# Attention values: per-head matrices against Wv, 64x64 weighing tiles and Wo

## What is computed

```
def mha(xq, ctx, wq, wk, wv, wo, bo):
    q, k, v = (heads of) xq @ wq, ctx @ wk, ctx @ wv
    attn = softmax(q k^T / sqrt(64))
    out = attn v                     # per head, then side by side: [.., 1024]
    return out @ wo + bo
x0 = layernorm(x)
h1 = adaln(x0);  y1 = mha(h1, h1, ...) + x0
h2 = adaln(y1);  y2 = mha(h2, context, ...) + y1
h3 = adaln(y2);  x1 = x + y2 + glu_ff(h3)
n  = layernorm(x1)
out = x1 + sum over the top 2 of 8 experts of score * (silu(a) * g) @ w2[e].T,   a, g = n @ w1[e].T
```

## Time and profile before

| | before |
|---|---|
| median of 3 runs | 2113.37 us (2111.95 to 2113.82) |
| profiled execution, first to last instruction | 2124.9 us |
| PE busy, weight loads busy | 2039.6 us, 1337.7 us |
| DVE, ACT, POOL busy | 1323.4, 1386.2, 1071.9 us |
| granted clock of PE, mean | 0.991 |
| DMA | 127.35 MB, 60 GB/s |

### The profile page before, as it was taken

How to read it: one execution, slowest core, us unless ns; L and a number is a source line. 1 busy time by engine, 2 the same in 40 slices (tenths; PEclk the granted TensorE clock), 3 DMA queues, 4 the chain that set the end, 5 groups by cost and what they waited for, 6 DMA issues and landing times. The chain is left out here.

```text
span 2124.9 us, 38735 instructions
## 1 busy us (share of the span) xinstructions
PE 2039.6 (96%) x11068; PEld 1337.7 (63%) x11068; DVE 1323.4 (62%) x3389; ACT 1386.2 (65%) x2659; POOL 1071.9 (50%) x1198
## 2 busy tenths in 40 slices
PE   7899999999999999999999999999999889899996
PEld 5455555555555555555555565555555558799996
DVE  5554657676767676767676666666656545455565
ACT  4566666676667676767676767676766666566663
POOL 2444444636363637363737373737363445556664
PEclk9999999999999999999999999999999999999998
DMA  4110111121111111111111111111122312222256
GB/s 153 45 26 25 50 35 51 46 50 45 49 45 50 46 53 45 49 45 49 45 49 45 49 45 51 47 48 52 44 54 64 96 48 57 58 56 72 60 185 215
DMA packets 136321, 127.35 MB, mean 60 GB/s; under 512 B 14665, under 2 KB 110569, under 8 KB 136234
## 3 DMA queue, kind: packets, MB, share of 16 engines
q1 hardware_dynamic: 127466, 109.11, 18.7%
q0 software_dynamic: 8768, 17.20, 2.5%
HBM read 86.63 MB, written 40.67 MB: 60 GB/s over the span
## 5 line engine op out<-in xcount | busy, mean ns | idle before, releaser
L1928 POOL TENSOR_TENSOR pr<-pr,sm 128x512 f32<-128x512 f32 x256 | 277.7, 1098 | 483.7 <-DVE sm L1462 483.7
L1126 ACT ACTIVATE kp<-ps 128x512 f32<-128x512 f32 x512 | 298.9, 601 | 179.5 <-PE ps L283 176.2
L834 PE MATMUL ps<-tt,V 128*128 128x512 f32 x768 | 380.3, 593 | 3.5 <-ACT tt L1126 3.5
L1452 DVE TENSOR_REDUCE mx<-ps 128x8 f32<-128x512 f32 x256 | 176.8, 691 | 306.3 <-PE ps L783 306.3
L1126 ACT ACTIVATE tt<-ps 128x512 f32<-128x512 f32 x512 | 275.2, 591 | 40.2 <-PE ps L813 39.6
L783 PE MATMUL ps<-kp,hf 128*64 128x256 f32 x2048 | 276.8, 392 | 6.9 <-DVE pr L1455 3.9
L283 PE MATMUL ps<-cT,M 128*128 128x512 f32 x768 | 262.0, 464 | 0.0
L783 PEld LDWEIGHTS ps<-kp,hf 128*64 128x64 f32 x2048 | 124.4, 136 | 196.9 <-DVE pr L1455 142.4
L1126 ACT ACTIVATE pt<-ps 128x512 f32<-128x512 f32 x256 | 153.6, 600 | 141.4 <-PE ps L795 139.1
L283 PE MATMUL ps<-hk,M 128*128 128x512 f32 x768 | 242.2, 438 | 0.0
L941 PE MATMUL ps<-xT,wt 128*128 128x128 f32 (+1 forms) x1728 | 221.9, 278 | 4.0 <-DVE wt L1753 4.0
(11 more groups left out here) (235 smaller groups left out, 3470.3 us busy)
## 6 DMA issues: line engine op xcount, KB each, us to landing
mod<-emb_s SPq DMA_DIRECT2D x96, 256.0 KB, 4.3
xr<-rows_s SPq DMA_DIRECT2D x144, 66.0 KB
cb<-y_s SPq DMA_DIRECT2D x32, 256.0 KB
x_in<-in_x_dram SPq DMA_DIRECT2D x16, 256.0 KB, 4.4
xn_s<-x_in SPq DMA_DIRECT2D x16, 256.0 KB, 2.1
res<-xn_s SPq DMA_DIRECT2D x16, 256.0 KB, 2.8
c_in<-in_ctx_dram SPq DMA_DIRECT2D x16, 256.0 KB, 4.7
y_s<-res SPq DMA_DIRECT2D x16, 256.0 KB, 2.0
```

The costliest lines, as they stand in the source:

```text
L834: mm = nc.tensor.matmul(psO[:], Vw[a][:, g * HG + head_at(h), :], tt[:, h, :], start=(g == 0 and h == 0), stop=ends)
L1126: return nc.scalar.activation(o, i, ACT.Copy)
L1452: nc.vector.tensor_reduce(mx[:, p % 2, :], heads(psS[p % 2][:]), AX_X, ALU.max).then_inc(max_done, 1)
L1928: tensor(v, v, sm[:, p, :].unsqueeze(2).broadcast_to([P, HG, 64]), ALU.mult).then_inc(prob_done, 1)
```

## The change

- Setup no longer multiplies Wv with Wo. Wv is kept as two float32r halves (WV0, WV1), Wo as it is (WO0, WO1).
- `values`: the values of a tile for eight heads, 3 matmuls of 512 columns, 4 tiles per unit; ACT copies them to vp.
- `weigh`: 64 matmuls per unit, each 64 rows, 64 stationary columns, 64 moving columns, in two groups (pairs) of four heads; the row halves go to two banks, the column halves to two halves of the partitions. ACT copies four banks to os.
- `project`: 16 matmuls with a 128x128 tile of os stationary and 128 columns of Wo moving; the result has rows as partitions, so oT, back1 and back2 of the attentions go. The bias is added to the residual rows by POOL (`add_bias`), the residual rows have tiles of their own (y1r, y2r).
- No float32r splits of tt and no copy h_tm, c_tm.
- Order on PE in a slot: four turns, two weighings, four scores, four projections, four values, then the key products with the stages and GLU products. The four turned tiles have banks of their own and ACT and DVE copy two each. Banks are dealt anew: scores in psum 0, 3, 4, 5, the feed-forward's sum in psum 6, the rings, now of keys and values, again 6, 6, 4 and 3 banks.

```diff
+            def values(i, u, t, bank):
+                a, g = divmod(u, 2)
+                src = hk if a == 0 else cT
+                mm3(bank[:], lambda k: src[:, k, t * P:(t + 1) * P], lambda k: WV[a][:, k, g * CT:(g + 1) * CT]).then_inc(v_done, 1)
             def weigh(i, u, pair):
-                for s in range(2):
-                    rows = slice(64 * s, 64 * s + 64)
-                    nc.tensor.matmul(pst[s][:], tm[rows, p, :], pt[rows, p % 2, :], start=True, stop=True).then_inc(t_done, 1)
+                if pair == 0:
+                    pe.wait_ge(vp_done, v_count(i, u, NT - 1))
+                    wait(turned(i, u, 0))
+                    wait(turned(i, u, 1))
+                else:
+                    for w in left_in(i, u, WEIGHED[3]):
+                        wait(w)
+                for t in range(NT):
+                    if pair == 0 and t > 1:
+                        wait(turned(i, u, t))
+                    if t == 0 or pair == 0 and t > 1:
+                        pe.sem_inc(seen, 1)
+                    for j in range(2):
+                        for odd in range(2):
+                            h = 4 * pair + 2 * j + odd
+                            g, c = divmod(h, HH)
+                            for e in range(2):
+                                keep = slice(64 * e, 64 * e + 64)
+                                mm = nc.tensor.matmul(WEIGHED[2 * pair + e][64 * odd:64 * odd + 64, 256 * j + 64 * t:256 * j + 64 * t + 64], vp[keep, t, 64 * h:64 * h + 64],
+                                                      pt[keep, t, c * P + 64 * g:c * P + 64 * g + 64], start=True, stop=True)
+                mm.then_inc(w_done, 1)
             def project(i, u, j):
-                    mm = nc.tensor.matmul(psO[:], Vw[a][:, g * HG + head_at(h), :], tt[:, h, :], start=(g == 0 and h == 0), stop=ends)
+                if j % 2 == 0:
+                    wait(weighed(i, u, j + 1))
+                for t in range(NT):
+                    mm = nc.tensor.matmul(psO[:, t * D:(t + 1) * D], os[:, j, t * P:(t + 1) * P], WO[a][:, HH * g + j, :],
+                                          start=(g == 0 and j == 0 and t == 0), stop=(g == 1 and j == HH - 1 and t == NT - 1))
...
             def slot(i, u):
+                if last:
+                    for p in range(NT):
+                        if p == NT - 1 and u == 3 and ok(i - 2) and not c_last(i - 2):
+                            pe.wait_ge(glu, FT * (i - 2) + 1)
+                        if p == NT - 1 and u == 0 and ok(i - 3):
+                            pe.wait_ge(glu, FT * (i - 2))
                         turn(li, lu, p)
+                if u == 0 and ok(i - 3) and not c_last(i - 3):
+                    glu_down(i - 3, FT - 1)
+                if last:
+                    for pair in range(2):
+                        weigh(li, lu, pair)
+                if here:
+                    for p in range(NT):
                         scores(i, u, p)
+                if last:
+                    for j in range(HH):
+                        project(li, lu, j)
+                if here:
+                    for t in range(NT):
+                        product("v", t)
                 for h in range(HG):
                     if then:
-                        next_key(h)
+                        product("k", h)
...
-                    if last and h >= 2:
-                        project(li, lu, h - 2)
```

On the other engines:

```diff
             def slot(i, u):          # ACT
+                if last:
+                    for p in (0, 2):
+                        turn_out(li, lu, p)
+                if u == 0 and ok(i - 3):
+                    out_glu(i - 3)
+                if last:
+                    for b in range(4):
+                        weighed_out(li, lu, b)
                 if here:
+                    for p in range(NT):
+                        exp(i, u, p)
+                    for t in range(NT):
+                        values_out(i, u, t)
...
             def slot(i, u):          # DVE
+                if last:
+                    for p in (1, 3):
+                        turn_out(li, lu, p)
                 for p in range(NT):
...
+                if here:
+                    total(i, u, 2)
+                    total(i, u, 3)
```

More of the change, by code:

```diff
@@ L777, in scores @@
                         pe.wait_ge(hx_hi[1], i)
-                if not (isinstance(n, int) and n < 2):
-                    pe.wait_ge(sub_done, n - 1)
+                elif live(*before(i, u)):
+                    wait(weighed(*before(i, u), p - 1))
+                bank = SCORED[p][:].rearrange("p (c s k) -> p c s k", c=HH, s=2)
                 for s in range(2):
                     cols = slice(p * P + 64 * s, p * P + 64 * s + 64)
-                    for j in range(2):
-                        mm = nc.tensor.matmul(psS[p % 2][64 * j:64 * j + 64, :].rearrange("p (h s k) -> p h s k", h=HH, s=2)[:, :, s, :],
-                                              hf[u // 2][:, cols], kp[:, j * HH:(j + 1) * HH, cols], start=True, stop=True)
-                        if s == 1:
-                            mm.then_inc(s_done, 1)
@@ L1005, in next_key @@
-                def next_key(h):
-                    if h < len(RINGS[u]):
-                        bank = RINGS[u][h]
-                        if last:
-                            for w in [(pt_done, 4 * seq(li, lu) + 4)] if bank is psT else [] if bank in psS else t_free(li, lu, 3 if bank is psH else 2):
-                                wait(w)
-                        if here and bank in psS:
-                            pe.wait_ge(sub_done, 4 * seq(i, u) + 4)
-                    keys(*after(i, u), h)
@@ new lines, in slot, with product @@
+                if last:
[3 more added lines that the diff above has]
+                    for p in range(NT):
+                        scores(i, u, p)
+                if last:
+                    for j in range(HH):
+                        project(li, lu, j)
+                def product(kind, x):
+                    made, banks = products(i, u), RINGS[u]
+                    j = made.index((kind, x))
+                    bank = banks[j % len(banks)]
+                    if j >= len(banks):
+                        for w in emptied(i, u, *made[j - len(banks)]):
+                            wait(w)
+                    elif bank in SCORED and here:
+                        pe.wait_ge(sub_done, 4 * seq(i, u) + SCORED.index(bank) + 1)
+                    elif bank in psS and isinstance(i, int) and i == NC:
+                        pe.wait_ge(eu_act, 3 * E)
+                    elif bank is psF and u < 2 and ok(i - 3):
+                        pe.wait_ge(f2_out, i - 2)
+                    if kind == "v":
+                        values(i, u, x, bank)
+                    else:
+                        keys(*after(i, u), x, bank)
@@ L1239, in out_glu @@
                 act.wait_ge(f2_done, FT * c + FT)
-                act.wait_ge(back1, c + 3 if ok(c + 2) else NC)
-                if c_last(c):
-                    act.wait_ge(back2, c + 1)
-                if not ok(c + 2):
+                if not first(c):
                     act.wait_ge(rt_done, c)
-                nc.scalar.activation(oT[:], psM[:], ACT.Identity, bias=b_2[:, 0:1]).then_inc(f2_out, 1)
+                nc.scalar.activation(oT[:], psF[:], ACT.Identity, bias=b_2[:, 0:1]).then_inc(f2_out, 1)
             def mix_out(c):
@@ L1536, in norm2 @@
                     dve.wait_ge(hx[1], 1)
[L1537 removed]
+                ln_norm(1, y1r, htm)
             def after_attn2(c):
[L1540 to L1544 removed]
+                dve.wait_ge(o_done[1], c + 1)
+                dve.wait_ge(bias_done[1], c + 1)
+                tensor(y2r[:], tiles3(psO[:]), y2r[:], ALU.add).then_inc(y2_done, 1)
             def norm3(c):
```

521 lines of the change are left out of this document (180 added, 341 removed).

## The result

| | before | after |
|---|---|---|
| median of the runs, us | 2113.6 (2111.95 to 2113.9) | 2163.9 (2160.9 to 2165.8) |
| profiled span, us | 2124.9 | 2164.1 |
| PE busy in the span | 96% | 88% |
| one round (4 slots with a unit each; 64 units in all), us | 104.85 | 109.27 |

The change makes the kernel slower: ratio 1.024 (95% interval 1.0227 to 1.0256), 2164 us where 2010 was predicted. Of the profile of the changed kernel, first the page: the busy times, and the row of the queue that brings in instructions (packets, MB, share); before, that queue's row was "q8 instruction: 40, 0.66, 0.1%".

A forecast was written before the change was run, and what follows sets the result against it. PE's own matmul stream was taken as the bound. Stream -172, dropped turns -14, setup -5, lost cover +88 sum to -103 us, giving a 2010 us median; forecast range 1960 to 2060 (chance 0.55), wider range 1940 to 2115.

The forecast's parts named there:

- the fourth of the places that lose cover: Slot starts: the weighing waits for the fourth turned tile's copy, 0.15 us each, 0.6 per round.
- h's split, psM: Slot 2's first up product waits for turned rows copied and split, 1.0 us; slot 0's three stages share bank psM, 0.5.
- PE's stream: PE's matmuls per unit: 22.74 us before, 20.05 after, 2.69 less, 172 us over 64 units.
- Rival 3: Slower: small matmuls don't overlap, a weighing takes 6.9 to 10.9 us, the kernel 2230 to 2480; chance 0.17.
- Instruction Overhead: Skill section: about 60 cycles overhead per matmul; taken to make each 64-column weighing instruction about twice as dear.
- The router's eight: Router's eight instructions of 24 columns keep PE busy 0.96 us, 0.12 each; read as a floor for small products.
- Rival 2: Waits take the whole gain: slots end up bound by the order on ACT and DVE, 2060 to 2115 us; chance 0.13.
- slot 3's ring of key banks: Argument for waits taking the gain: slot 3's ring has three banks, and values join the queue there.
- PSUM Bottleneck: Skill section cited for waits taking the gain: tiling speeds up TensorE but not the evacuation.
- Its price: Claim that 2.7 us more wait per unit than now would return the whole gain.
- The lost cover in the GLU: Slot 3: less fill between up products, 1.6 us short twice and about 0.8 before the last down product, 4.0 per round.
- Setup: Before the rounds: a 32-instruction product and eight transposes per attention go, two Wv splits come; 5 us gain.

The follow-up runs named there:

- dve_order: Changed kernel with three slot-ending DVE stages moved behind the next slot's two copies of turned tiles: 2081.4 us, 0.979 of before; 0.982 in a second group.
- before_unrolled2: Kernel before with rounds 4 to 14 written out on PE instead of looped, other engines unchanged: 2111.7 us, 0.9997 of before.
- after_same_chip: The changed kernel again, nothing edited, to share a chip with its variants: 2157.4 us, 1.022 of the kernel before.
- split_weighing2: Changed kernel with DVE's three slot-ending stages behind its copies, and the weighing block cut in two around the first head's scores: 2064.5 us, 0.977 of before.
- dve_order_unrolled: Changed kernel with DVE's three slot-ending stages behind its copies, and rounds 4 to 14 written out on PE: 2076.8 us, 0.977 of before.

## Why the prediction was wrong

**The step that failed** is the fourth of the places that lose cover: "Slot starts: the weighing waits for the fourth turned tile (0.2 + 0.69 after its turn): 0.15 each, 0.6 per round." It took the copy at its own duration. In the profile after, 2.85 + 1.15 + 2.58 = 6.58 us of a round are waits for these copies, eleven times as much, because the stages that end a slot on DVE are ahead of them (965.47 to 968.07, 988.90 to 993.19). The kernel before weighed one tile at a time, with turns and scores between the earlier trace rows. The prediction said that what counts is order, and then followed only PE's order. dve_order confirms the step by itself: with nothing but DVE's order changed, its round is 8.2 us shorter (109.27 to 101.10), and 5.6 of that are these waits, 6.58 down to the 0.95 that is left ahead of the weighing at 439.44, for ACT's copy. The other 2.6 are, in the main, half-clock work and the pause of 1.45, which that round happens not to have. (6.58 x 14.5 rounds and the 4.5% gained both come to 95 us; the agreement is luck.)

**The sum by rounds.** Predicted: 104.85 - 4 x 2.69 - 0.86 + 6.1 = 99.3 us. Measured 109.3, and 10 us by 14.5 rounds are 145 of the 154 us by which the median missed.

| per round, us | predicted | measured after |
|---|---|---|
| PE's own work at full clock | 93.2 | 93.2 |
| waits for turned copies | 0.6 | 6.6 |
| GLU | 4.0 | 1.6 |
| h's split, psM | 1.5 | 0 |
| keys' copies ahead of the turns | 0 | 1.0 |
| pauses of the instruction supply | 0 | 3.7 |
| the same work at clock 0.50 | 0 | 2.9 |

The first line after is the busy time 96.07 less the last line, which is 3.33 - 2.10 plus 3.58 - 1.95. That it equals the predicted 93.2 is partly luck: the weighings are 4 x 0.48 = 1.9 below the forecast, so other terms are as much above, and which wasn't traced. A matter of 0.3 us of short gaps is in no line. The 3.7 are 2.28 + 1.45, the GLU's 1.6 are 0.75 + 0.82.

**Point by point.**
- PE's stream: right. Turns 1.87 predicted, 1.95 measured (at 989.45); weighing 2.5 and 2.02; scores 3.63 and 3.61; projection 3.65 and 3.59; values 2.80 and 2.88. The weighing is 0.016 us per instruction against 0.053 alone (0.43 for 512 columns, divided by 8): 3.4 at a time.
- Rival 3, small matmuls one at a time: refuted by that. So is the estimate after "Instruction Overhead" of the Trainium skill (TensorEngine Tiling (Array Packing)), which made 3.4 us at four at a time and 6.9 at two. The prediction had mis-sized it besides: an instruction of 64 columns alone is 0.053 us, 127 cycles at 2.4 GHz, so 60 cycles more, the figure of that section of the Trainium skill, make it half as dear again and not twice. By this estimate the block is 2.5 us at four at a time, and the measured 2.02 is under that too. Small instructions did cost something here, but in the supply of all of them and not in each. (The router's eight, which the prediction read beside this as 0.12 each by duration, are 0.10 each from start to start, 957.14 to 957.95; no term rests on it.)
- Rival 2, waits take it all: nearest to what came, and its words "bound by the order on ACT and DVE" name the cause. But it looked for it in slot 3's ring of key banks and not at the slot starts, its times end at 2115, and its sign isn't met: waits for copies of kp, vp, os or pt over 150 us, where the copies ahead of weighings (87.4) and turns (14.4) make 102 of the 174. The rule that it cites, "PSUM Bottleneck" of the Trainium skill (same page), is evacuation that doesn't keep pace with a faster TensorE, and that is not this case: DVE is 66% and ACT 62% busy in the round (72.18 and 67.53 of 109.27), and dve_order, with just as much to evacuate, gets rid of most waits. It was order, not throughput. Its price, that 2.7 us of wait more per unit would return the whole gain, was about right: 12.85 a round are 3.2 per unit, with the clock's 2.9 a round on top, and the loss follows.
- The lost cover in the GLU was overpriced: 4.0 against 1.6. So were h's split and psM, 1.5 against none. Together they make up for 3.9 us a round of what the slot starts were short by.
- The instruction supply wasn't on the list. The count, 505 to 1048 matmuls in a round, followed from the prediction's own numbers; its "no stretch of the trace issues instructions this densely" was used against the overlap only.
- Setup: 5 us of gain were predicted. The first scores start at 44.23 us, where before had 42.59, so there is none up to there.
- Of the clock nothing was said: that a pause is paid again in the work after it. dve_order, with fewer long waits, has a granted clock of 0.98 in its round where after has 0.97.

**What is left.** Even in order the change gives 0.977 to 0.982 where the prediction had 0.951. Splitting on one chip: the first expert product starts at 1748.97 us in before_unrolled2 (as fast as before), 1787.33 in after_same_chip and 1683.24 in split_weighing2: 66 us are gained up to there, setup and attention stage. The expert stage then takes 376.5 us against 360.2, giving 16 back. Waits of PE in the expert stage, in split_weighing2 (4.5 us in after_same_chip):

```profile
PE ps L911 <- DVE wt L1651: 10.1, 7, 3.2
```

Expert weights are now waited for more, probably since the work ahead of them is shorter; that is 5.6 of the 16, and the rest wasn't traced. Of the 37 us between 66 and the predicted 103 the supply's pauses, 25.4 + 11.6, are the largest term that the runs show. That the numbers are equal is no proof: other terms were off both ways (too much for the GLU, nothing for the keys' copies, setup), and no run took the supply's pauses away and left the work.

## What to carry to other kernels

When an edit turns interleaved short steps into blocks, follow the queue of every engine that feeds the block: what is ahead of the copy there when it becomes due, by start times and not by its own duration. Count the instructions too: a block of very many short ones can be fast in itself and leave the loop's body too large to stay, which costs at the jump and, most of all unrolled, in the middle of the block. And before removing one wait or some work, ask what waits behind it: here the 25 us saved at the jump came back, 20 of them in pauses a little later. Last, split a row of waits by where they stand: "issue" was a late copy ahead of the block and a late instruction inside it.

## What the runs showed of the hardware that I had not expected

- TensorE takes in its instructions in 16 KB transfers once a loop's body is large: none between 800 and 1010 us at 1009 or some 1330 matmuls and loads a round, 21 at 2096. The limit lies somewhere between the last two. At 2096 it pauses 2.3 to 2.8 us ahead of the body's first block (25 us in all over ten jumps); the kernels whose body stays show no such pause.
- Written out instead (dve_order_unrolled), as many a round give pauses inside the dense blocks, most of some 0.38 us, the longest 1.7, 30.4 us in all; 1009 a round, written out, give none.
- 128 instructions (64 float32 products) of 64x64 over 64 columns, spread over the four quarters of the array, take 2.02 us, 0.016 each (993.98 to 996.00 in the changed kernel).
- After waits of 2.85 and 2.28 us the granted clock was 0.50 and 0.51 in the following 2.6 and 3.5 us; after one of 2.58 (993.98) the same block ran in 2.10, at 1.00. So a wait of this length sometimes costs another 1.2 to 1.6 us, and the runs don't show what decides it.
